# A causal mask on GpSimd: one product with a stored mask, or two selections by row and column number

## What is computed

```python
q = q.reshape(b, H, g, n, DH)                 # 8 key heads, 2 query heads for each
sim = jnp.einsum('bhgid,bhjd->bhgij', q, k)
sim = jnp.tanh(sim / SOFTCLAMP) * SOFTCLAMP
sim = sim * DH ** (-0.5)
causal = jnp.triu(jnp.ones((n, n), dtype=bool), 1)
sim = jnp.where(causal, neg, sim)
attn = jax.nn.softmax(sim, axis=-1)
out = jnp.einsum('bhgij,bhjd->bhid', attn, v)  # summed over the two query heads
```

## Time and profile before

| | us |
|---|---|
| three runs | 2081.46, 2081.14, 2079.12 |
| median | 2081.14 |
| profiled execution | 2070.81 |
| its span, first to last instruction | 2069.1 |
| TensorE busy | 1838.8 (89%) |
| VectorE busy | 1195.2 (58%) |
| ScalarE busy | 877.6 (42%) |
| GpSimd busy | 609.9 (29%) |
| the masks on GpSimd, 128 of them | 167.3 |

### The profile page before, as it was taken

How to read it: one execution, slowest core, us unless ns; L and a number is a source line. 1 busy time by engine, 2 the same in 40 slices (tenths; PEclk the granted TensorE clock), 3 DMA queues, 4 the chain that set the end, 5 groups by cost and what they waited for, 6 DMA issues and landing times. The chain is left out here.

```text
span 2069.1 us, 31611 instructions
## 1 busy us (share of the span) xinstructions
PE 1838.8 (89%) x11768; PEld 1586.8 (77%) x11768; DVE 1195.2 (58%) x2023; ACT 877.6 (42%) x1076; POOL 609.9 (29%) x452
## 2 busy tenths in 40 slices
PE   3698898897987998998899899779999999999997
PEld 2598798897976877777787778668787787877876
DVE  6788878888865776777667677421341414314141
ACT  3554554544435664666367366322222222212221
POOL 3212223223150231332122122232433334333332
PEclk9799999998998999999999999889999999999999
DMA  9122311213111000200200020060000000000000
GB/s 120 54 77 97 118 75 53 89 75 145 49 44 50 22 22 9 84 22 15 77 22 15 8 70 22 8 267 1 21 21 0 20 0 20 20 0 21 1 11 11
DMA packets 32213, 95.89 MB, mean 46 GB/s; under 512 B 18630, under 2 KB 18758, under 8 KB 26569
## 3 DMA queue, kind: packets, MB, share of 16 engines
q1 hardware_dynamic: 32076, 94.00, 14.5%
HBM read 81.37 MB, written 24.15 MB: 51 GB/s over the span
## 5 line engine op out<-in xcount | busy, mean ns | idle before, releaser
L573 PE MATMUL conv<-w_hi,x_hi 128*128 128x368 f16 (+5 forms) x1320 | 355.0, 278 | 4.2 <-issue 4.0
L573 PE MATMUL conv<-w_lo,x_hi 128*128 128x368 f16 (+5 forms) x1320 | 355.7, 278 | 0.0
L573 PE MATMUL conv<-w_hi,x_lo 128*128 128x368 f16 (+5 forms) x1320 | 354.4, 278 | 0.0
L835 POOL TENSOR_TENSOR probs<-probs,mask 128x512 f32<-128x512 f32 x128 | 167.3, 1307 | 440.6 <-ACT probs L909 440.6
L1327 ACT ACTIVATE raw_c<-ring,sh 128x512 f32<-128x512 f32 x128 | 88.2, 689 | 371.3 <-PE ring L1424 371.2
L1115 PE MATMUL mixed<-v,probs 128*128 128x65 f32 x1536 | 201.6, 282 | 41.4 <-DVE parts L995 41.2
L1115 PEld LDWEIGHTS mixed<-v,probs 128*128 128x128 f32 x1536 | 185.8, 195 | 56.9 <-issue 40.2
L1289 POOL TENSOR_TENSOR ha_lo<-raw_c,ha_hi 128x512 fp32r<-128x512 f32 x128 | 165.1, 1290 | 210.0 <-DVE ha_hi L1339 210.0
L1424 PE MATMUL ring<-ha_hi,wh 128*128 128x512 f32 x512 | 208.7, 408 | 16.9 <-POOL ha_lo L1289 16.9
L1424 PE MATMUL ring<-ha_lo,wh 128*128 128x512 f32 x512 | 205.2, 401 | 0.0
L1339 DVE CAST ha_hi<-raw_c 128x512 fp32r<-128x512 f32 x128 | 80.7, 631 | 213.2 <-ACT raw_c L1327 211.0
(11 more groups left out here) (153 smaller groups left out, 3757.1 us busy)
## 6 DMA issues: line engine op xcount, KB each, us to landing
xt<-x_columns_in SPq DMA_DIRECT2D x12, 1163.0 KB, 5.2
xp<-x_patches_in SPq DMA_DIRECT2D x12, 1152.0 KB, 8.9
hidden_words<-hidden_weights_in SPq DMA_DIRECT2D x8, 1408.0 KB, 8.7
words<-hidden_words SPq DMA_DIRECT2D x32, 352.0 KB, 3.1
wh<-hidden_words SPq DMA_DIRECT2D x2, 4096.0 KB, 21.2
tokens<-total SPq DMA_DIRECT2D x4, 1024.0 KB, 4.6
lines<-tokens SPq DMA_DIRECT2D x4, 1024.0 KB, 5.5
h<-tokens SPq DMA_DIRECT2D x4, 1024.0 KB, 7.4
```

The lines of the kernel that those rows point to most:

```text
L573: ins = pe.matmul(out, xs[:, c, RI - 1 - i:RI - 1 - i + NR, :, x].rearrange("p r g -> p (r g)"), w, start=(t == 0), stop=(t == len(terms) ...
L835: pool.tensor_tensor(diag, diag, both, ALU.mult).then_inc(s_mask, 1)
```

## The change

The product with the stored mask is replaced by a `settle` and two selections. Each selection works in place on one diagonal square of both query heads, 2 x 128 columns: it keeps an element where column − row is at least 0 and writes 0 elsewhere. The second one signals `s_mask`. The tile `mask` is still built and no longer read.

```diff
--- before.py
+++ after.py
@@ -830,9 +830,12 @@
                     elif kind == "score":
                         n = step[1]
                         pool.wait_ge(s_exp, g * NH + n + 1)
-                        diag = probs[:, n % 4].rearrange("p m (b i) -> p m b i", b=3)[:, :, 0:3:2]
-                        both = mask[:].rearrange("p (m b i) -> p m b i", m=1, b=1).to_broadcast([P, 2, 2, P])
-                        pool.tensor_tensor(diag, diag, both, ALU.mult).then_inc(s_mask, 1)
+                        settle(pool, s_settle)
+                        for jb in range(2):
+                            diag = probs[:, n % 4, :, 2 * jb * P:(2 * jb + 1) * P]
+                            ins = pool.affine_select(out=diag, in_=diag, compare_op=ALU.is_ge, fill=0.0, base=0,
+                                                     pattern=[[0, 2], [1, P]], channel_multiplier=-1)
+                        ins.then_inc(s_mask, 1)
                 if run.before:
                     pool.wait_ge(s_aggr, g + 1)
                     settle(pool, s_settle)
```

## The result

| | before | after |
|---|---|---|
| median of the runs, us | 2080.7 (4 runs) | 2045.35 (4 runs, 2042.93 to 2055.7) |
| profiled execution, us | 2070.81 | 2046.93 |
| its span | 2069.1 | 2045.2 |

The ratio is 0.9841, 95% interval 0.9806 to 0.9876: the change makes the kernel 1.2 to 1.9% faster, 35 us by the medians. Forecast were 16 us and a range down to 2054. The sign and the path were right; the size forecast was less than half of the measured one.

The account below looks back on a forecast made before the run. TensorE was taken to bound the attention stage, idling on VectorE instructions that GpSimd's mask holds up. Shorter holds gain 12 or 21 us, taken as 16, off the median: 2081 − 16 = 2065 us, range 2054 to 2086.

Parts of the forecast that it names:

- What bounds the kernel: Attention stage: TensorE sets the pace, idling 41.2 us for VectorE's `parts`; GpSimd's mask delays VectorE but is not waited for.
- The price of a selection: GpSimd, 256 columns: 0.40 us each, the pair 0.80 (0.77 to 1.18) where the product took 1.27.
- The first rival: Selections don't hold VectorE's ports, so whole stretches go: 23.5 us in all, 2057 us; chance 0.12.
- The second: Rival: pair as long as the product, or freed time meets another wait; no measurable change, 2079 us; chance 0.13.
- the third: Rival: selections from 0.64 us each make VectorE wait longer; slower kernel, mostly 2086 to 2111 us; chance 0.15.
- the gain on the waits: TensorE's waits behind stretched VectorE instructions shrink: 3.3 or 5.6 us a group, 12 or 21 us over 3.67 groups.
- let in: VectorE gets in between the two selections: a stretch falls by 0.87 us, 5.6 us a group.
- kept: GpSimd keeps its hold through the pair of selections: a stretch falls by 0.47 us, 3.3 us a group.
- the sum: Gains on the listed TensorE waits of one group, times 3.67 groups: 12 or 21 us, taken as 16.
- The settle: One 17 ns semaphore instruction a head on GpSimd's queue: costs nothing, hidden by slack.
- The slack of 1.6 us: Last heads: time from the mask's end to the product that reads it, at its tightest; hides added delay.

Follow-up runs that it names:

- e5: Changed kernel plus the old 512-column product on a spare tile, behind the two selections and their signal: 2101.75 us, ratio 1.0112 to the kernel before.
- e4: Kernel before with only the semaphore increment added ahead of the product: 2081.92 us, ratio 1.0046.
- e7: Changed kernel with four selections of 128 columns in place of its two of 256: 2033.47 us, ratio 0.9784 to the kernel before.

## Why the prediction was wrong in its size

**What bounds the kernel** held. The mask was not on the path, its exclusion of VectorE was, and e5 shows it: with the mask early and a product back, the wait for `parts` is 43.0 us.

**The price of a selection** was forecast at 0.40 us and measured at 0.409. The pair takes 0.77 and not 0.80, for the overlap. The first rival (no hold) fell: `o` is still late by up to 0.25 us. The second (no change) and the third (slow selections, from 0.64 us) fell with the duration.

**The step that failed is the gain on the waits, "12 or 21 us, I take 16, about the middle, because nothing shows who gets the ports between two selections".** VectorE gets them, at 661.62 in the timeline after. An `o` now ends 0.83 us less late than before (0.25 for 1.08) and a chain 0.71 (0.33 for 1.04), near the 0.87 of "let in" and far from the 0.47 of "kept". From 655 us on TensorE's waits fell by 21.1 us for `parts` and 4.7 for `kt` and grew by 3.1 for the mask, 22.7 in all, where the sum had 16; the span of the profiled execution fell by 23.9 (2069.1 to 2045.2).

**That the upper value, 21, comes out so near is partly luck.** The sum counted six waits of a group, 7.9 us, and put the others at nothing. In 820 to 997 us TensorE waited 11.5 us for `parts` and 1.5 for `kt`; after, 5.8 and none. These 7.2 us are more than the 5.6 that the sum had at best, so waits that it did not list shrank too. The 1.2 us of new waits for the mask in that window hide the difference.

**What the sum left out** is the rest up to 28 to 35 us of the medians. It took the difference off the median, and the profiled execution (2070.81) as an ordinary one 10 us off by a constant. That one was at the low end of what the kernel before does (2070 to 2092 us over all its runs) with a clock of 0.954, where the median of its runs is 0.948 to 0.949; the profiled one of after (2046.93, 0.951) was in the middle of its own. The forecast priced an idle microsecond at one microsecond and had no term for the clock. So the profiled pair understates the gain: TensorE's idle time fell by 27.8 us, 5 more than the waits named above (some of that outside the attention stage), while its busy time rose by 3.9, at the lower clock. What else lies between these 28 us and the 35 of the first pair of medians, no run shows.

**Smaller steps.** The settle was costed at nothing, hidden by slack; e4 shows 0.1 us a head on the start of the mask, and 0.2 to 0.8% on the kernel before. The hidden part was the mask's readiness, the visible one the end of the hold, which shifts as well. The slack of 1.6 us was true of the old timing only: with TensorE earlier, five mixes wait for the mask, up to 0.8 us. And a chain meets both selections, which the forecast did not have (it let the second go free); in the chain shown it costs 0.15 us.

## What to carry to other kernels

An instruction on GpSimd that no one waits for can still set the pace, if small VectorE instructions with two SBUF inputs run in a chain ahead of something that TensorE needs: compare the shortest and the longest duration of each VectorE line, and see what GpSimd does beside the long ones. There, when they run over many columns, short GpSimd instructions are worth more than few; the same squares in four selections of 128 columns are 12 us faster than in two of 256, side by side, though GpSimd works longer for them (1.9 to 2.5% under the kernel before by two measurements), and eight give nothing more. And before a difference is taken off a median, look where the profiled execution lies among the runs: here it was 10 us and six thousandths of clock away from it.

## What was not expected of the hardware

- The hold ends before the instruction does: a VectorE instruction is late by the duration of the GpSimd instruction less 0.12 to 0.20 us, and between two that follow each other directly VectorE gets its turn. The Trainium skill, "SBUF — State Buffer", section "SBUF: two separate sides", has the pair of ports locked for the whole instruction. By the trace this is nearly so (1.08 of 1.277 us). The lock is stated there for one instruction, and the traces agree that it does not last through a sequence.
- A GpSimd instruction of 1.64 us on 8 columns (L829) holds up none of the Newton steps beside it by more than 0.03 us.
- It also works the other way. A selection that meets `bits` of VectorE at 837.93 in the kernel after takes 1.121 us in place of 0.409, and in e7 one of the three from 699.40 us on takes 1.272, in place of 0.292, beside the product of 1.30 us in `scale`.
- A semaphore increment of 17 ns between a wait and a GpSimd instruction starts that instruction 0.10 us later (e4; in the changed kernel the first selection starts 0.163 us after the exp, the product before 0.078).
- The cost of a selection grows far slower than its width: 0.238 us for 64 columns, 0.292 for 128, 0.409 for 256; the product goes 0.457, 0.734 and 1.277 for 128, 256 and 512.
